# Row maxima of an attention block taken from 128-row operands instead of 64 rows, with the operands' copies issued two units earlier

## The reference

```python
xn = silu(group_norm(x, gn_scale, gn_offset))      # 32 groups
qkv = einsum('bxyc,cd->bxyd', xn, w_qkv)           # 512 -> 1536
q, k, v = to_heads(...)                            # 8 heads of 64 channels
sim = einsum('bhdi,bhdj->bhij', q * 64 ** -0.5, k) # 1024 x 1024 a head
attn = softmax(sim, axis=-1)
out = einsum('bhij,bhdj->bhid', attn, v)
out = einsum('bxyc,cd->bxyd', out, w_out) + b_out
return out + x
```

## Time and profile before

| | before |
|---|---|
| runs, median (lowest to highest) | 4288.79 us (4285.77 to 4290.70) |
| profiled execution, span | 4293.1 us |
| mean granted TensorE clock | 0.973 |
| PE busy | 4020.1 us (94%) |
| DVE busy | 3129.0 us (73%) |
| ACT busy | 2837.5 us (66%) |
| POOL busy | 1627.1 us (38%) |

### The profile page before, as it was taken

One profiled execution on the slowest core, in us unless ns is written; L12 is line 12 of the kernel. 1 busy time (PEld: TensorE's weight loads), 2 busy tenths in 40 slices (PEclk: granted clock), 3 DMA queues, 4 the chain that ended last, 5 costly groups with the idle time before them and its releaser, 6 DMA issues.

```text
span 4293.1 us, 94034 instructions
## 1 busy us (share of the span) xinstructions
PE 4020.1 (94%) x32844; PEld 2046.2 (48%) x32844; DVE 3129.0 (73%) x5216; ACT 2837.5 (66%) x3202; POOL 1627.1 (38%) x1226
## 2 busy tenths in 40 slices
PE   3999999899999999999999999999999999999997
PEld 1444545444454444445445454444544444444443
DVE  5687777767777677776777777677776777768774
ACT  2576676667667676676766766676676776767664
POOL 1243343433334333343433434334343333434333
PEclk8999999999999999999999999999999999999999
DMA  2111212122031120311212121220311203111121
GB/s 76 30 46 48 60 29 75 31 60 61 16 90 31 50 56 18 88 31 53 53 34 72 31 74 32 54 66 16 85 36 48 58 16 90 31 53 53 31 63 36
DMA packets 119497, 212.44 MB, mean 49 GB/s; under 512 B 19536, under 2 KB 19536, under 8 KB 118992
## 3 DMA queue, kind: packets, MB, share of 16 engines
q1 hardware_dynamic: 118992, 205.86, 17.8%
HBM read 71.57 MB, written 33.55 MB: 24 GB/s over the span
## 4 chain that ended last, share of the span: by engine, by line
PE 66%; issue 17%; POOL 7%; DVE 6%; ACT 3%; DVEq 0%; POOLq 0%; DMA 0%; SPq 0%; ACTq 0%
PE SD L929 29%; PE PV L1052 12%; PE TP L943 9%; PE ST L1018 6%; PE ST L1019 6%; POOL Pl L492 5%; DVE Pl L795 2%; DVE mx L741 2%; PE SD L992 1%; POOL xn L479 1%; PE TP L951 1%; ACT QK_hi L553 1%; PE SD L986 1%; ACT Ph L594 1%; ACT V L558 1%
## 5 line engine op out<-in xcount | busy, mean ns | idle before, releaser
L741 DVE TENSOR_REDUCE mx<-TP 128x1 f32<-128x512 f32 x2048 | 1349.9, 683 | 412.1 <-PE TP L943 403.2
L591 ACT ACTIVATE P<-ST,cns 128x1024 f32<-128x1024 f32 x1024 | 1143.6, 1117 | 598.4 <-PE ST L1019 551.0
L492 POOL TENSOR_TENSOR Pl<-P,Ph 128x1024 f16<-128x1024 f32 x512 | 1117.1, 2182 | 795.2 <-ACT Ph L594 795.1
L594 ACT ACTIVATE Ph<-ST,cns 128x1024 f16<-128x1024 f32 x1024 | 1138.8, 1112 | 0.0
L1052 PE MATMUL PV<-V,Ph 128*128 128x129 f16 (+2 forms) x10240 | 888.7, 213 | 34.8 <-POOL Pl L492 22.0
L1052 PEld LDWEIGHTS PV<-V,Ph 128*128 128x128 f16 x10240 | 769.5, 98 | 303.6 <-issue 268.9
L1052 PE MATMUL PV<-V,Pl 128*128 128x65 f16 x8192 | 853.8, 194 | 0.0
L1018 PE MATMUL ST<-Q,K 128*128 128x512 f16 x2048 | 796.4, 389 | 48.9 <-issue 48.9
L1019 PE MATMUL ST<-Q,K 128*128 128x512 f16 x2048 | 796.3, 389 | 0.0
L943 PE MATMUL TP<-QK_hi 64*128 64x512 f16 x2048 | 729.6, 392 | 61.2 <-DVE mx L741 42.0
L929 PE MATMUL SD<-xn,wq 128*128 128x512 f16 x3072 | 733.7, 381 | 25.2 <-POOL xn L479 16.0
(11 more groups left out here) (92 smaller groups left out, 2828.9 us busy)
## 6 DMA issues: line engine op xcount, KB each, us to landing
work<-in_x SPq DMA_DIRECT2D x128, 256.0 KB, 2.8
Q<-QK_hi SPq DMA_DIRECT2D x256, 128.0 KB, 2.6
K<-QK_hi SPq DMA_DIRECT2D x256, 128.0 KB, 2.8
res<-in_x SPq DMA_DIRECT2D x128, 256.0 KB, 3.2
out<-res SPq DMA_DIRECT2D x128, 256.0 KB, 2.3
K<-QK_lo SPq DMA_DIRECT2D x128, 128.0 KB, 2.7
Q<-QK_lo SPq DMA_DIRECT2D x128, 128.0 KB, 2.6
V<-in_L_conv_w_qkv SPq DMA_DIRECT2D x1, 3072.0 KB, 10.7
```

The costliest lines, as they stand in the source:

```text
L492: nc.gpsimd.tensor_tensor(Pl[:, v % 4, :], P32[:, v % 2, :], Ph[:, v % 4, :], ALU.subtract).then_inc(lo_pool, 1)
L591: nc.scalar.activation(P32[:, v % 2, :], ST[:, v % 2, :], ACT.Exp, scale=cns[:, 0:1])
L594: nc.scalar.activation(Ph[:, v % 4, :], ST[:, v % 2, :], ACT.Exp, scale=cns[:, 0:1]).then_inc(exp_done, 1)
L741: nc.vector.reduce_max(mx[:, hh, qb, kh:kh + 1], TP[:, cnt.top_bank], AX.X).then_inc(top_drained, 1)
```

## The change

1. The maxima multiply `Q1` by `K1` (128 rows: q high with k high, plus q high with k low) in place of `QK_hi` (64 rows). The number of matmuls, their columns and the reductions on DVE stay.
2. So the first maximum of a head waits for the six copies of its head (`placed[hh]`). The scores no longer wait for `placed`, since the maxima came first. The wait for the drain of `qk` goes from the maxima.
3. `PLACE_AT` goes from 10 to 8.
4. `TOP_LEAD` = 6: the tops of head h run in units 8h-6 to 8h+1 instead of 8h-8 to 8h-1. The first head of a pair thus begins its maxima at unit 10 of the step before.
5. The score's wait for the shift is counted from the shift itself (`cnt.shifted[q]`).

```diff
+TOP_LEAD = 6
 def top_uses(step, u, last=False):
-    w, hh = u % 8, u // 8
-    if last and step == 3 and hh == 1:
+    head, w = divmod(16 * step + u + TOP_LEAD, 8)
+    if last and head == HEADS:
         return []
     done = sum(TOPS_PER_W[:w])
-    return head_tops(*((step, 1) if hh == 0 else ((step + 1) % 4, 0)))[done:done + TOPS_PER_W[w]]
-TOPS_SINCE_SHIFT = (7, sum(TOPS_PER_W[:4]))
+    return head_tops(head // 2 % 4, head % 2)[done:done + TOPS_PER_W[w]]
+def top_slot(u):
+    return (u + TOP_LEAD) % 8
-PLACE_AT = 10
+PLACE_AT = 8
+AHEAD = sum(TOPS_PER_W[:TOP_LEAD])
-            + [use for t in range(TB) for use in [("v", t)] + head_tops(0, 0)[9 * t // 4:9 * (t + 1) // 4]])
+            + [use for t in range(TB) for use in [("v", t)] + head_tops(0, 0)[2 * t:min(2 * t + 2, AHEAD)]])
...
-            def top_use(use, cnt):
+            def top_use(use, image, cnt):
                 bank = cnt.top_bank
                 wait(pe, top_drained, cnt.top - 1)
                 if use[0] == "max":
                     _, pair, hh, qb, kh = use
-                    r = rows_of(hh)
+                    slot = head_slot(pair, hh)
                     if qb == kh == 0:
-                        wait(pe, side_drained, cnt.mark["qk"])
-                    ins = nc.tensor.matmul(TP[:, bank], QK_hi[r, pair % 2, 0, bass.ts(qb, P)],
-                                           QK_hi[r, pair % 2, 1, bass.ts(kh, HALF)],
+                        pe.wait_ge(placed[hh], PLACED * (4 * image + pair + 1))
+                    ins = nc.tensor.matmul(TP[:, bank], Q1[:, slot, bass.ts(qb, P)], K1[:, slot, bass.ts(kh, HALF)],
                                            start=True, stop=True)
...
                     if v % 4 == 0:
-                        pe.wait_ge(top_drained, cnt.top - TOPS_SINCE_SHIFT[q])
-                    if v % 8 == 0:
-                        pe.wait_ge(placed[head % 2], PLACED * (4 * b + head // 2 + 1))
+                        pe.wait_ge(top_drained, cnt.shifted[q])
...
-                    place = TOP_PLACES[u % 8 == 7][late]
+                    place = TOP_PLACES[top_slot(u) == 7][late]
```

More of the change, by code:

```diff
@@ L145, in follows_split, with image_of_tops @@
     return any(use[0] in SPLIT for use in side_before(step, u, first, last))
+def image_of_tops(b, step, u):
+    return b + (16 * step + u + TOP_LEAD) // (8 * HEADS)
 def image_of(use, b, step):
@@ L178, with __init__ @@
                  "top": HEADS * 18, "shifts": 2 * HEADS}
-    def __init__(self, side=0, hi=0, top=0, shifts=0, mark=None):
+    def __init__(self, side=0, hi=0, top=0, shifts=0, mark=None, shifted=(0, 0)):
         self.side, self.hi, self.top, self.shifts, self.top_bank = side, hi, top, shifts, 0
+        self.shifted = list(shifted)
         self.mark = dict(mark or {"qk": 0, "v": 0, "ot": 0})
@@ L189, in passed @@
                 self.shifts = self.shifts + 1
+                self.shifted[use[3]] = self.top
             return
@@ L199, in later @@
         then = Count(self.side + n["side"], self.hi + n["hi"], self.top + n["top"], self.shifts + n["shifts"],
-                     {kind: at + n["side"] for kind, at in self.mark.items()})
+                     {kind: at + n["side"] for kind, at in self.mark.items()},
+                     [at + n["top"] for at in self.shifted])
         then.top_bank = self.top_bank
@@ L818, in step @@
                     late = follows_split(s, u, first, last)
-                    ahead = TOPS_AHEAD[u % 8 == 7][late]
+                    ahead = TOPS_AHEAD[top_slot(u) == 7][late]
                     for use in tops[:ahead]:
@@ L1064, in step @@
                     late = follows_split(s, u, first, last)
-                    place = TOP_PLACES[u % 8 == 7][late]
+                    place = TOP_PLACES[top_slot(u) == 7][late]
                     for use in tops[:place[0]]:
-                        top_use(use, cnt)
+                        top_use(use, image_of_tops(b, s, u), cnt)
                     if not (first and v < 2):
@@ L1099, in _ @@
                 if use[0] in ("max", "shift"):
-                    top_use(use, cnt)
+                    top_use(use, 0, cnt)
                 else:
```

## The result

| | before | after |
|---|---|---|
| runs, median (lowest to highest) | 4289.74 us (4285.77 to 4291.78) | 4405.02 us (4402.78 to 4408.79) |
| ratio, with its 95% interval | | 1.0273 (1.0258 to 1.0287) |
| profiled execution, span | 4293.1 us | 4407.1 us |
| mean granted TensorE clock | 0.973 | 0.951 |

The forecast was 4208 us, in a range of 4140 to 4275. The change costs 115 us where 80 were to be gained. Of the rivals, C (slower by the copies, 4327) has the sign, and not the size. The median of before is of four runs here, one more (4291.78) than stands ahead of the prediction.

The account below looks back on a forecast made before the run. PE's instruction list was taken as the bound. Stretches removed (-19.4 us an image) against copy waits and clock gave -4.3 an image, -69 over 16; with first image, last image and prologue -80, so 4208 us, range 4140 to 4275.

Parts of the forecast that it names:

- C: Rival: unit 10's wait for copies, with low clock behind it, outweighs the gain; 4327 us, chance 0.08.
- stretches collected: Per image, 97 stretches of 64-row maxima on PE vanish, 19.4 us, less 0.6 in step 1 and 0.3 in step 2.
- shift of the tops: Unit 8 of step 0, DVE behind after moving V: one top fewer saves 0.7 us of wait an image.
- copies: 7.1 + 2.6 + 4.2 + 1.0: Costs an image: step 0 stall 7.1 and low clock 2.6; step 1 longer units and uncounted stretches 4.2, clock 1.0.
- The 0.2 us: PE's price for each stretch of 64-row maxima, however long: 0.09 us on the way in, 0.10 out.
- what is not collected: Stretch gain lost an image: 0.6 us where ACT binds in step 1, 0.3 for DVE's reductions in early step 2.
- Rival B: The gain turns into waits for DVE's reductions, a fifth of 19.4 us (3.9 an image); 4270 us, chance 0.16.
- the two microseconds in units 7 to 12 of step 2: DVE binds there, but the shift relieves it of 1.4 us, so the ten stretches' 2.0 us count as collected.
- Step 0: First maximum of unit 10 waits for copies held behind store and load: stall 7.1 us, then 2.6 of low clock.
- Step 1: Stall of 3.7 us; last x load lands late, units 9 to 11 +3.0, +4.2 with uncounted stretches; clock +1.0.
- Step 2: The 2.7 us stall for copies in unit 10 hides behind DVE: 0 (0 to 2.7).
- A: Rival: the clock recovers at once after the new idle, only stalls count; 4154 us, chance 0.22.

Follow-up runs that it names:

- 1: Kernel before with its maxima multiplying all 128 rows of QK_hi instead of one head's 64, nothing else moved: 4106.93 us, ratio 0.957.
- 9: Kernel after with maxima over all 128 rows of QK_hi, tops six units ahead, copies at unit 10, no maximum waiting for a copy: 4195.15 us, ratio 0.9782.
- 10: Same as 9, with the move of V at unit 4 of step 0 instead of unit 7: 4143.09 us, ratio 0.9655.
- 6: Same as 2, with the move of V at unit 4 of step 0 instead of unit 7: 4337.44 us, ratio 1.0105.
- 7: Kernel after with thirty overwritten 512-column matmuls ahead of the wait for copies in unit 10 of step 0: 4391.77 us, ratio 1.0233.
- 2: Kernel after with maxima from 64 rows of QK_hi again and PLACE_AT 10, leaving only the tops' shift by two units: 4392.88 us, ratio 1.0241.
- 5: Kernel after with copies issued earlier and split in two parts, and the move of V at unit 4 of step 0 instead of 7: 4154.83 us, ratio 0.9684.

## Why the prediction was wrong, by its own steps

| us an image | booked | measured |
|---|---|---|
| stretches collected: -19.4 + 0.6 + 0.3 | -18.5 | -11.9 (1 against before) |
| shift of the tops | -0.7 | +5.9 (9 against 1) |
| copies: 7.1 + 2.6 + 4.2 + 1.0 | +14.9 | +14.3 (after against 9) |
| sum | -4.3 | +8.3 |

**The price of a stretch was right, what it brings was not.** Two steps failed, by 6.6 us an image each. The 0.2 us stood in the rows and went in full. The first step that failed is "what is not collected", 0.9 us, which should have been 7.5: in 1 the waits grew by 10.1 us an image (15.2 to 25.3), and 2.7 of low clock went. It asked where DVE is busy nearly all of a stretch of 16 or 19 us, and found two places. But a wait needs no busy engine: a maximum's bank comes free only 0.683 us after the last but one was filled, a `Pl` is due at a fixed point of its unit, and each unit has its own slack for that. When the units shrink by 0.2 to 0.6 us such slack is used up in many of them. Rival B priced this at 3.9 us, about half, and had the right engine but only a part of the mechanism: it named waits for the reductions, and those grew by 21 us over the run in 1, 1.3 an image, while those for `Pl` grew from 31.0 to 78.9 us. Also the two microseconds in units 7 to 12 of step 2 were taken as collected, on the argument that the shift of the tops relieves DVE: these units take 28.1 us in after and 27.4 in 9, against 27.4 before. The shift does relieve DVE there, by 1.0 us (28.4 in 1, 27.4 in 9), but that only makes up for what the 128 rows had lost.

**The shift of the tops was the second step that failed.** It was booked as "one top fewer saves 0.7 us" in unit 8 of step 0, where in fact the unit went from 6.08 to 8.6 us. With the shift of the tops DVE drains two maxima in unit 7 where it had drained one spread shift (the cast of L746), so that the move of V comes one reduction later behind the `OT` ahead of it, 2.94 us in place of 2.34; POOL comes only 0.27 us later. That moved POOL's lead over the copy from 0.18 to 0.51 us, and turned a cost of POOL, which PE did not have to wait for there, into one of DVE, for which PE waits: 2.9 us an image, 9 against 10. The row that gave the warning was in the trace before: one `Pl` of POOL of 3.39 us among those of 2.13, under the copy of V. I had read DVE's and PE's rows around unit 8, not POOL's. The remaining 3.0 to 3.4 us (10 against 1, 6 against before) are scattered waits, low clock and, at 64 rows only, the seven stretches more; which wait costs how much of them stays open.

**The copies were right in step 0, and in sum.** Step 0: a stall of 7.05 us on average for 7.1, and 1.9 of low clock for 2.6; 0.8 of wait stood in that unit anyway (9), so 8.1 us net for 9.7. The 2.6 came from one place with 6 us of work at the low clock; here the mean is 3.5 us. Step 1: 5.4 us for 5.2 in units 10 to 12 (after against 9), but composed in another way: a stall of 4.1 and low clock of 2.3, less 1.0 of waits that 9 has there anyway, with the last `xt` not waiting for its load at all. The forecast let the landing of that load set the length of units 9 to 11, which it does not; that the sum fits is in part luck. Step 2: the stall of 2.46 hides behind DVE, as said; it brings 0.7 us of low clock and waits. Step 3: none. Only rival C saw that these could outweigh the gain, and it took nearly all of the gain as collected; A (the clock stays up) falls with the rows at 0.51 and with 7.

So of the 12.6 us by which the image came out longer than forecast, 6.6 are of the overestimated gain, 6.6 of the shift, and -0.6 of the copies.

## What to carry to other kernels

A gain on the bounding engine is worth, unit by unit, no more than the distance to the next wait, and a mean busy share of 73% on the next engine does not tell that distance: go through the waits of each unit, and book a share of the gain as lost where there are many small ones. Before moving anything past a long DVE instruction, look for GpSimd instructions of unusual length beside it; one that is 1.3 us too long and harmless can become a DVE instruction that is 1.5 us too long and not harmless. When a matmul gets a new operand, its wait moves to the first reader in PE's order, and the queue that produces the operand has to be read from its last blocking entry on: here moving the copies from behind one store's landing was worth 126 us, more than the whole loss.

## What the runs showed of the hardware

**This DVE copy and this GpSimd operation exclude each other.** The copy of 128x4160 fp16 takes 1.22 us, POOL's `Pl` 2.13 us. When they overlapped, one kept its duration and the other ended after about the sum, with nearly the same gap in 14 or more of the 16 images: POOL started 0.18 us ahead (before) or 0.29 (kernel 1), and POOL took 3.39 or 3.50 us; 0.51 ahead (kernels 2, 9 and after), and the copy took 2.72. The sum works out: 2014.03 + 2.13 + 1.22 = 2017.38, and the copy ended at 2017.26. With no overlap (5, 6, 10) both are at their own length. The Trainium skill ("SBUF — State Buffer", section "SBUF: two separate sides") says that the port pair shared by VectorE and GpSimd is an exclusive lock for the whole instruction, held by whichever starts first of a GpSimd operation and a VectorE operation that uses the pair. The durations agree; "starts first" doesn't by the profile's start times, since POOL began 0.18 us earlier and still lost.

The trace of before shows a second such pair. DVE's `ms` (128x4), which takes 0.23 us, lasts longer than 0.3 us in 99 of its 256 places, and the 69 that lie beside a `Pl` of POOL with nine tenths of their length or more have a median of 1.03. One of them, with POOL's row beside it:

```profile
2034.24 1.03 DVE L733 TENSOR_SCALAR ms<-mx,cns 128x4 f16<-128x4 f32 x1
...
2033.11 2.13 POOL L492 TENSOR_TENSOR Pl<-P,Ph 128x1024 f16<-128x1024 f32 x1
```

It ends at 2035.27, POOL's `Pl` at 2035.24. With the tops six units ahead 15 or 16 of the 256 are so long. The reductions don't meet POOL in this way: 497 of them lie beside a `Pl` of POOL to the same extent in before, and take 0.68 us like the others.

**64-row matmuls between 128-row ones.** A stretch of them costs 0.09 us on the way in and 0.10 out in before, and nothing when the same matmuls have 128 rows (1, 9, after). In kernel 2, with 104 stretches, the price stays.

**The clock after a wait.** Behind 6.6 to 7.35 us of idle in unit 10 of step 0 of after PE worked 2.6 to 6.0 us at 1.2 GHz, and then at 2.4 GHz; with 0.70 us of idle in the same place it stayed at 2.4 GHz (7). Behind the idle of 2.63 us in unit 8 the granted clock fell in 11 of 15 images of after, and the unit took 8.6 to 9.1 us; in the other four, image 7 among them, it stayed up, and the unit took 7.38.
